# Filler matmuls on TensorE, a packed type table, and another way to the one-hot of the destination's type, in a two-layer graph network on one core

## What is computed

```
h  = relu(layernorm(x))
# layer 0: gated messages from dst to src, mean over each src, layernorm
gate = silu(edge_attr @ W1.T + b1) @ W2.T + b2
gate = gate + sum(emb[z[src]] * (emb[z[dst]] @ adaptW.T))      # z: node type, 119 kinds
msg  = gate * h[dst] * (cw(dist) * node_mult[dst])
agg  = segment_sum(msg, src) / segment_sum(node_mult[dst], src)
x    = x + layernorm(h + agg) * gamma + beta
h  = relu(layernorm(x))
# layer 1: a two-layer product for each edge, picked by the edge's type
h2   = relu(h @ weight1[rel] + bias1) @ weight2[rel]           # for h[src]
x    = x + relu(segment_sum(h2 * norm, dst) + bias2)
```

## Time and profile before

| | us |
|---|---|
| median of 3 runs | 1531.99 (1529.84 to 1539.69) |
| span of the profiled execution, first to last instruction | 1526.4 |
| stage one: first add of POOL, last add issued | 212.7, 741.6 |
| stage two: first gather, last add issued | 743.5, 1415.3 |
| last stage, loads and stores | 1418 to 1526 |
| busy over the span: PE, DVE, ACT, POOL | 1130.4, 1319.3, 668.1, 1026.1 |
| mean granted clock of PE | 0.613 of full speed |

### The profile page before, as it was taken

One profiled execution on the slowest core, in us unless ns is written; L12 is line 12 of the kernel. 1 busy time (PEld: TensorE's weight loads), 2 busy tenths in 40 slices (PEclk: granted clock), 3 DMA queues, 4 the chain that ended last, 5 costly groups with the idle time before them and its releaser, 6 DMA issues.

```text
span 1526.4 us, 20418 instructions
## 1 busy us (share of the span) xinstructions
PE 1130.4 (74%) x5198; PEld 831.4 (54%) x5198; DVE 1319.3 (86%) x3932; ACT 668.1 (44%) x1627; POOL 1026.1 (67%) x809
## 2 busy tenths in 40 slices
PE   5889899989999899881068888887878887775000
PEld 2767677777777777771035555555555555554000
DVE  6999999999989998980289999998989899888599
ACT  2444444544445444540155555555555555554000
POOL 7655667777877787566667787877777777766000
PEclk9666655655556655655575656655565556666555
DMA  7999986666666656642445666555555555554899
GB/s 225 307 324 327 328 236 157 153 146 143 142 166 149 149 139 143 155 101 11 100 120 143 166 167 156 140 138 137 136 139 127 132 131 138 138 127 81 328 400 398
DMA packets 154391, 268.73 MB, mean 176 GB/s; under 512 B 73818, under 2 KB 90411, under 8 KB 153380
## 3 DMA queue, kind: packets, MB, share of 16 engines
q1 hardware_dynamic: 78228, 223.53, 43.8%
q0 software_dynamic: 68992, 24.64, 18.5%
q10 hardware_dynamic: 7056, 19.27, 3.1%
HBM read 194.33 MB, written 112.55 MB: 201 GB/s over the span
## 4 chain that ended last, share of the span: by engine, by line
PE 34%; DVE 20%; DMA 19%; POOL 12%; issue 10%; ACT 3%; SPq 1%; POOLq 0%; DVEq 0%; ACTq 0%
PE ps_m L572 10%; POOL agg L485 8%; DMA t<-agg,src_all 6%; PE ps_m L661 6%; PE ps_qs L572 6%; DMA lows<-low 4%; PE ps_k L647 3%; DVE same L858 2%; DMA agg<-y,once 2%; DMA agg<-ysq,once 2%; DVE t L1074 2%; DVE x L1070 2%; PE ps_k L559 2%; PE ps_k L560 2%; PE ps_qs L610 1%
## 5 line engine op out<-in xcount | busy, mean ns | idle before, releaser
L521 POOL DMA_INDIRECT agg<-sums,once x196 | 312.7, 1595 | 103.5 <-issue 79.8
L443 POOL DMA_INDIRECT nodes<-in_table,dst_all x196 | 194.9, 995 | 102.2 <-issue 51.7
L512 POOL DMA_INDIRECT t<-agg,src_all x196 | 191.5, 977 | 66.1 <-issue 53.9
L572 PEld LDWEIGHTS ps_m<-msg,same 128*128 128x128 f32 x980 | 200.8, 314 | 29.0 <-issue 29.0
L572 PE MATMUL ps_m<-msg,same 128*128 128x48 f32 x980 | 208.5, 398 | 1.0 <-issue 1.0
L647 PE MATMUL ps_k<-h_t,rw_sb 56*128 56x256 f32 x588 | 122.7, 536 | 114.0 <-ACT hid L742 91.3
L572 PEld LDWEIGHTS ps_qs<-msg,same 128*128 128x128 f32 x980 | 183.6, 289 | 2.1 <-DVE msg L950 2.1
L572 PE MATMUL ps_qs<-msg,same 128*128 128x49 f32 x980 | 180.7, 363 | 2.0 <-DVE msg L950 2.0
L485 POOL DMA_INDIRECT agg<-x,once x84 | 137.4, 1635 | 43.9 <-issue 21.7
L647 PEld LDWEIGHTS ps_k<-h_t,rw_sb 56*128 56x128 f32 x588 | 62.9, 242 | 157.1 <-ACT hid L742 115.2
L559 PE MATMUL ps_k<-types_lo,low_hot 128*128 128x392 bf16 x196 | 95.7, 488 | 52.7 <-DVE low_hot L833 51.0
(11 more groups left out here) (149 smaller groups left out, 2620.2 us busy)
## 6 DMA issues: line engine op xcount, KB each, us to landing
agg<-in_both SPq DMA_DIRECT2D x14, 2758.0 KB, 15.3
t<-agg SPq DMA_DIRECT2D x49, 784.0 KB, 5.3
kept<-kept_out SPq DMA_DIRECT2D x49, 404.0 KB
kept_in<-kept SPq DMA_DIRECT2D x49, 404.0 KB, 3.5
agg<-bias_rows SPq DMA_DIRECT2D x49, 384.0 KB
out<-t ACTq DMA_DIRECT2D x49, 384.0 KB, 5.8
rows<-in_src_rows SPq DMA_DIRECT2D x49, 256.0 KB, 4.2
rows<-in_dst_rows SPq DMA_DIRECT2D x49, 256.0 KB, 3.2
```

Source lines behind the costliest of these rows:

```text
L443: pool.indirect_dma_start(nodes[s][:, t, :], None, table, bass.IndirectOffsetOnAxis(ap=dst_all[:, c:c + 1], axis=0)).then_inc(nodes_in[b % ...
L512: pool.indirect_dma_start(t2[b % T2S][:, t, :], None, wide, bass.IndirectOffsetOnAxis(ap=src_all[:, c:c + 1], axis=0)).then_inc(ends_in[b ...
L521: pool.indirect_dma_start(agg1, bass.IndirectOffsetOnAxis(ap=once1[b % LAG1][:, t:t + 1], axis=0), sums1[b % LAG1][:, t, :], None, compute ...
L572: last = mm(ps[:, t * width:(t + 1) * width], kept_same[:, at:at + P], m[:, v, :], start=(v == t), stop=(v == TILES - 1))
```

## The change

Three edits.

**The type table holds two types in a word.** Types of column n and column n + 196 are joined to one 16-bit pattern: a small multiple of 128 for the one, added to the other, with an offset that makes the bits a bf16 number. The lookup's products are 196 columns wide rather than 392, and so is `type_of`. What it accumulates is a float whose bits hold both types. DVE then shifts those bits right by 16 or 23 (`shift_all`, by whether the high part of src is at least 196), and masks 7 bits: two operations on 128x4 for each block (`zs_bits`, `zs_now`). The stored types are 8 higher than before, which `iota_type[:, ZBASE:]` takes up.

**The one-hot of z[dst] is made by PE and ACT.** DVE casts the four types of a partition to bf16 (128x4, `zd_bf`). PE multiplies each column, broadcast to 128 columns, with a bf16 identity: all rows of `ps_t` then hold the types of 128 edges. ACT squares the difference to the row's number (`apart`) and takes relu(1 - that): 1 where equal, 0 elsewhere. The 128x476 comparison of DVE (L884) and the copy of ACT (L705) are gone.

**`keep_clock`.** Products of a bf16 identity with itself, 512 columns, whose result nobody reads. In stage one there are ten for each block: three ahead of the first two lookups, one behind them, three inside `sums_within`, and one each ahead of `h1`, behind it, and behind `centred`. They write the unused bank. In stage two there are six for each round: three inside `sums_within` and three behind m1. They write `ps_k[1][:, 1]`, in which k1 has been computed; so `sums_within` now also waits for `relu1_done` of the same round.

```diff
-            types_lo = sb1("types_lo", [P, 2, NHI], BF16)
+            types_lo = sb1("types_lo", [P, 2, NPK], BF16)
...
-                pool.wait_ge(S["onehot_done"], step + 1)
+                pool.wait_ge(S["zd_done"], step + 1)
...
+            spin = ident_bf[:, :].unsqueeze(1).to_broadcast([P, TILES, P])
+
+            def keep_clock(ps, n):
+                for _ in range(n):
+                    mm(ps, ident_bf[:, :], spin, start=True, stop=True)
...
-            def sums_within(ps, width, kept_same, m):
+            def sums_within(ps, width, kept_same, m, ps_spin):
                 for t in range(TILES):
                     for v in range(t, TILES):
+                        if v == t and t > 0:
+                            keep_clock(ps_spin, 1)
...
             for b in range(NBLOCK):
+                keep_clock(ps_idle, 3)
                 if b + 1 < NBLOCK:
                     lookup(b + 1, 0)
                     lookup(b + 1, 1)
-                pe.wait_ge(S["onehot_done"], b + 1)
-                need(pe, S["onehot_t_done"], b)
+                keep_clock(ps_idle, 1)
+                pe.wait_ge(S["zd_done"], b + 1)
+                need(pe, S["apart_done"], b)
                 for t in range(TILES):
-                    last = nc.tensor.transpose(ps_t[0:NTYPE, t * P:(t + 1) * P], onehot[:, t, :], ident[:, :])
-                last.then_inc(S["turned_t_done"], 1)
+                    last = mm(ps_t[:, t * P:(t + 1) * P], zd_bf[:, t:t + 1].to_broadcast([P, P]), ident_bf[:, :], start=True, stop=True)
+                last.then_inc(S["zd_wide_done"], 1)
...
                 last.then_inc(S["gate_done"], 1)
+                keep_clock(ps_idle, 1)
                 if b + 1 < NBLOCK:
                     h1(b + 1)
+                    keep_clock(ps_idle, 1)
                     centred(b + 1)
+                    keep_clock(ps_idle, 1)
...
                     pe.wait_ge(S["m1_copied"], f + 1)
-                    sums_within(ps_sums1, H, same[f % 2], msg1).then_inc(S["sums1_done"], 1)
+                    need(pe, S["relu1_done"], min(e + 1, NBLOCK))
+                    sums_within(ps_sums1, H, same[f % 2], msg1, ps_idle1).then_inc(S["sums1_done"], 1)
...
                     last.then_inc(S["m1_done"], 1)
+                    keep_clock(ps_idle1, 3)
...
-                act.wait_ge(S["turned_t_done"], b + 1)
+                act.wait_ge(S["zd_wide_done"], b + 1)
+                A(apart[:, :], ps_t[0:NTYPE, :], ACT.Square, bias=minus_type[:, :]).then_inc(S["apart_done"], 1)
+                act.wait_ge(S["apart_done"], b + 1)
                 need(act, S["q_done"], b)
-                nc.scalar.copy(onehot_t[:, :], ps_t[0:NTYPE, :]).then_inc(S["onehot_t_done"], 1)
+                A(onehot_t[:, :], apart[:, :], ACT.Relu, scale=-1.0, bias=1.0).then_inc(S["onehot_t_done"], 1)
...
-                V.tensor_tensor(onehot[:, :, :], each(iota_type[:, :], TILES),
-                                node[:, :, H + 1:H + 2].bitcast(I32).to_broadcast([P, TILES, NTYPE]),
-                                ALU.is_equal).then_inc(S["onehot_done"], 1)
+                V.tensor_copy(zd_bf[:, :], node[:, :, H + 1:H + 2].bitcast(I32).rearrange("p t o -> p (t o)")).then_inc(S["zd_done"], 1)
...
+                dve.wait_ge(S["zsel_done"], (b + 1) * TILES)
+                V.tensor_tensor(zs_bits[:, :], zs_all[:, at:at + TILES].bitcast(I32), shift_all[:, at:at + TILES],
+                                ALU.logical_shift_right).then_inc(S["zshift_done"], 1)
...
+                V.tensor_scalar(zs_now[:, :], zs_bits[:, :], P - 1, None, ALU.bitwise_and).then_inc(S["zs_done"], 1)
```

More of the change, by code:

```diff
@@ L40 @@
 assert NHI * LO == NP
+NPK = NHI // 2
+assert NPK * 2 == NHI
+ZBASE = 8
+assert NTYPE + ZBASE <= P
 CW1 = NREL * H
@@ L207, in build @@
             hdst = sb1("hdst", [P, TILES, H])
-            onehot = sb1("onehot", [P, TILES, NTYPE])
+            zd_bf = sb1("zd_bf", [P, TILES], BF16)
+            minus_type = sb1("minus_type", [NTYPE, 1])
+            apart = sb1("apart", [NTYPE, BE])
             onehot_t = sb1("onehot_t", [NTYPE, BE])
@@ L250, in build @@
         ps_c = ps_k[0]
-        ps_l = [ps_k[1][:, a, 0:NHI] for a in range(2)]
+        ps_l = [ps_k[1][:, a, 0:NPK] for a in range(2)]
         ps_h1 = ps_m[0:H, :]
+        ps_idle = ps_k[0][:, 1, :]
+        ps_idle1 = ps_k[1][:, 1, :]
         ps_gate = ps_s[:, BE // 2:BE // 2 + TILES * H]
@@ L581, in sums0 @@
                 pe.wait_ge(S["glog_done"], b + 1)
[L582 removed]
+                sums_within(ps_s, AW, same[b % 2], msg[b % 2], ps_idle).then_inc(S["sums_done"], 1)
             h1(0)
@@ L805, in _ @@
             dve.wait_ge(S["types_in_done"], 16)
-            V.tensor_copy(types_lo[:, :, :].rearrange("p k n -> p (k n)"), types_in[:, :])
+            of_two = types_in[:, :].rearrange("p (k two n) -> p k two n", k=2, two=2)
+            V.scalar_tensor_tensor(out=types_two[:, :, :], in0=of_two[:, :, 1, :], scalar=float(P), in1=of_two[:, :, 0, :],
+                                   op0=ALU.mult, op1=ALU.add).then_inc(S["types_set"], 1)
+            dve.wait_ge(S["types_set"], 1)
+            V.tensor_scalar(types_lo[:, :, :].rearrange("p k n -> p (k n)").bitcast(U16),
+                            types_two[:, :, :].rearrange("p k n -> p (k n)"), float(ZBASE * P + ZBASE), None, ALU.add)
             dve.wait_ge(S["idx_in"], 32)
@@ L810, in _ @@
             dve.wait_ge(S["keys_set"], 2)
-            V.tensor_copy(hi_all[:, :], hi_int[:, :]).then_inc(S["keys_set"], 1)
+            V.tensor_scalar(upper[:, :], hi_int[:, :], float(NPK), None, ALU.is_ge).then_inc(S["keys_set"], 1)
+            dve.wait_ge(S["keys_set"], 3)
+            V.scalar_tensor_tensor(out=hi_all[:, :], in0=upper[:, :], scalar=-float(NPK), in1=hi_int[:, :], op0=ALU.mult,
+                                   op1=ALU.add).then_inc(S["keys_set"], 1)
+            V.tensor_scalar(shift_all[:, :], upper[:, :], 7.0, 16.0, ALU.mult, ALU.add).then_inc(S["keys_set"], 1)
             dve.wait_ge(S["pool_set"], POOL_SET)
```

37 lines of the change are left out of this document (24 added, 13 removed).

## The result

The change made the kernel slower. The changed kernel takes 1586.96 us (median of 4 runs, 1573.67 to 1592.65), the kernel before on the same chip 1530.91 us (4 runs, 1517.64 to 1539.69): a ratio of 1.0359, interval [1.0288, 1.043].

A forecast was written before the change was run, and what follows sets the result against it. POOL was taken to set stage one's end and nearly bound stage two. Gains of 3 us at the first add, 3 at stage one's end and 7 in stage two made -13: 1531.99 to 1519 us, range 1492 to 1546.

The forecast's parts named there:

- Stage one, first add: First 14 blocks, bound by DMA at share 0.98: 3 us gained, POOL's first add between 206 and 212 us.
- rival C: Fill stretch of stage one not bound by DMA, so DVE's gain arrives: -24 us, 1508 us; chance 0.12.
- End of stage one: POOL sets it; shorter blocks give some three more POOL blocks the short wait: 3 us taken, -6 with the first add.
- DVE gains 1.0 us a block: Stage one: narrower type_of and the cast replacing the comparison shorten DVE's work by 1.0 us a block, hidden behind 212 us.
- Stage two, price of the three inner fillers: Fillers between k2 and m1 add 0.7 to 1.3 us at half clock in a waiting round; 1.3 taken.
- Stage two, share of waiting rounds at full clock: Stage two: three in five waiting rounds taken to find full clock, giving -7 us over 24 pairs of rounds.
- The gain of 1.35 us a pair: Stage two: at full clock POOL takes back its wait ahead of the adds, 1.65 - 0.30 = 1.35 us.
- the hole ahead of k2: Stage two: DVE's wait for gathers leaves PE idling 3.77 us ahead of k2, which the six fillers don't fill.
- Rival D: Stage two: clock stays at half in waiting rounds, +1.3 us a pair between k2 and m1, +31 less 6, 1557 us; chance 0.14.
- a microsecond on the path costs a microsecond for each pair of rounds: Stage two: the path from gathers landed to next gathers spans two rounds, so a microsecond is half a microsecond a round.

The follow-up runs named there:

- e12_no_fillers: Changed kernel without any filler in either stage and without the wait for relu1_done: packed types and new one-hot alone; 1536.67 us, ratio 1.002 to the kernel before.
- e2_fill_two_only: Kernel before with only stage two's six fillers and the wait for relu1_done added; 1583.49 us, ratio 1.0361.
- e7_before_later: Kernel before, but SP issues the two loads of a later chunk only when the gathers in flight have landed; 1515.6 us, ratio 0.9933.
- after: The changed kernel with all three edits, against the kernel before; 1586.96 us, ratio 1.0359.
- e8_late_copy: Kernel before with one more ACT operation, a copy of 128x768 nobody reads, ahead of stage two's copy of sums; 1609.02 us, ratio 1.0547.
- e4_behind_only: Changed kernel with only the three fillers behind m1 in stage two, no inner ones and no wait for relu1_done; 1541.38 us, ratio 1.0038.
- e1_no_fill_two: Changed kernel without stage two's six fillers and the wait for relu1_done, stage one keeping all of the change; 1523.53 us, ratio 0.9972.

## Why the prediction was wrong

I predicted 1519 us in 1492 to 1546, and the median is 1586.96. By its steps:

- **Stage one, first add: inside its range, by no gain that can be told.** 211.5 us, inside 206 to 212, but the other traces on two chips have 209.9 to 213.2 with the change in stage one and 211.9 to 213.8 without; the 3 us did not come. The DMA share is still 0.98 and blocks 1 to 13 take 13.47 us against 13.55, so the gain on DVE did not arrive there, as row and bound said, and rival C is out.
- **End of stage one: the number met, by luck.** -6 us forecast, -5.7 in the one pair of traces, but no gain in the four traces with the change against the four without on the two chips above. DVE's busy time fell by 62 us where some 50 were named. But the blocks became 2.0 us shorter rather than 1.0. The last copy of sums came at 621.8 us, 70 us earlier, and POOL was 107 us late by then (its first add of the last block is at 728.78). POOL hid all of it. The step "DVE gains 1.0 us a block" priced busy time as if it were pace. Without fillers, and with PE at half clock throughout, a block gained 0.2 (`e12_no_fillers`); 1.8 came with the fillers and the clock that they brought.
- **Stage two, price of the three inner fillers: inside its bounds.** 0.7 to 1.3 us at half clock, 0.86 measured (4.50 to 5.36), 0.29 us each. The sum took 1.3, half as much again.
- **Stage two, share of waiting rounds at full clock: wrong.** "I take three in five" was 0 of 18. The gain of 1.35 us a pair that rested on it never came. The text had named the hole ahead of k2 that six fillers don't fill, and then did not let it decide. Full clock came only in rounds that don't wait (9 of 18 have fast sums), and there POOL has no use for it. The windows of the round shown above (the wait, the sums, m1; then m1 of the round before, which had no wait) have it in the column of the clock:

```profile
1250.65:1257.80 7.15, 1.08 (x4) 0.50 (x4) 3.37 (x9) 1.95 (x5) 6.24 (x4) 0.62 0.69 183
1257.80:1263.10 5.30, 5.30 (x25) 4.95 (x23) 5.26 (x20) 3.13 (x9) 4.08 (x5) 0.50 0.40 84
1263.10:1265.90 2.80, 2.80 (x13) 1.25 (x12) 2.73 (x3) 0.28 (x2) 0.16 (x1) 0.50 0.10 18
1244.80:1246.20 1.40, 1.40 (x13) 0.77 (x12) 1.36 (x8) 0.92 (x4) 1.09 (x2) 1.00 0.85 174
```

- **Stage two, what a late copy sets off: missing.** Rival D had the sign, the place and the signature (sums over 5 us, rounds over 13.3), with +31 us and 1557 us. Measured are 50.6 us. The step that failed is that a microsecond on the path costs a microsecond for each pair of rounds. A pair went from 26.48 to 28.82 us, +2.34. Of this 0.86 is the fillers and 3.82 - 2.35 = 1.47 is the landing of the gathered rows, together 2.33; that they add up so closely is partly luck, since the kernel before had 13 waiting rounds and not 18, and m1 became 0.3 us shorter. The later copy moved the last gather from 0.10 to 0.78 us behind the load's issue. The earlier trace rows showed DVE's 1.78 us of waiting, and I took it for a fixed delay of the gather. The queue of SP stood in no step of the prediction, though the loads are released by the very engine that waits.
- **That it is the loads** rests on three pairs of kernels that differ in when SP issues the two loads, and with them what stands behind them in its order, and in nothing else: 1.0359 and 1.0038 with the fillers (two chips, each beside its own kernel before; `e2_fill_two_only`, on the chip of the second, has 1.0361), 1.0547 and 1.0117 with ACT's delay, 1 and 0.9933 with neither. Landing falls from 3.82 and 4.64 us to 1.79 and 1.68.
- **Why a landing gets so long** behind 1188 KB of loads, the trace shows in good part. The gathers are on the software queue and the loads on SP's, and the rows were there 4.53 us after the wide load's issue, where the profile's page has 5.1 us as this load's own median to landing (KB, us):

```profile
t<-agg SPq DMA_DIRECT2D x49, 784.0 KB, 5.1
```

  The trace also holds every DMA record with its start, length and size. One gather is 16 records of 3136 bytes, the load of kept values 128 of 3232, the wide one 128 of 6272. Means for a block's last gather, in us from the end of its issue:

| rounds | load's first record | gather's first record | gather's last end | length of one |
|---|---|---|---|---|
| `e7_before_later`, not waiting | 2.61 | 0.71 | 1.23 | 0.25 |
| before, waiting | 1.01 | 0.70 | 2.01 | 0.56 |
| after, waiting | 0.39 | 2.06 | 3.30 | 0.17 |
| `e8_late_copy`, waiting | -0.04 | 2.63 | 4.11 | 0.14 |

  With the load a little behind, the gather starts on time and its records take twice as long. With the load ahead, the gather starts late: when its first record starts, 88 of the 128 records of kept values have started on average in `after` and 109 in `e8_late_copy`; all 128 have started in 6 and in 13 of their 18 waiting rounds. So the lateness is for the most part waiting behind the load of kept values. In one round of `after` the gather's first record came at 1.80 us though none of the load's had started, so something ahead of the transfers takes part too; what, no run shows. The Trainium skill (DMA: Bandwidth & Descriptors, section "Queues, rings and completion order") says that each DMA engine goes round the queues that have work and takes a whole packet, typically some 9 to 17 descriptors, before it changes. If a record is a descriptor and they are spread evenly, the load of kept values has 128 / 16 = 8 for each of 16 engines, so by that page the wait could be for one such packet; the trace doesn't tell which engine or packet a record belonged to, and none of the runs changed the size of the load.
- **What stays open**: why the kernel before has 13 waiting rounds, `e4_behind_only` ten and `e1_no_fill_two` none, and whether the wait for `relu1_done` adds anything alone.

## What to carry to other kernels

Before putting work on a path, look at what the end of that path releases and what other queue is released by its neighbour at about the same time: here 0.86 us on PE cost 2.3 us, as it moved the last of four small gathers behind a megabyte of loads for a later chunk. Of the 3.6% about 1% was the delay itself, which stays when the loads come later; the rest was what it set off. Fillers for the clock pay only where the clock is high in the rounds that are waited for, and where the engine behind has time to take back; read both from the trace for waiting and other rounds apart, since their mean (0.73 here) hides that the rounds that matter are at 0.5. And a load for a later block can be held back until the current block's small transfers have landed: one wait on SP gave 0.7% [0.4, 1.0] with no work removed on the kernel before, and nothing on `e1_no_fill_two`, where no round waited.

## What the runs showed of the hardware

- Four indirect gathers landed 1.5 to 1.7 us after the last one was issued with no load just ahead of them, 2.35 us when the load was issued 0.10 us ahead of the last one's end, 3.82 us at 0.78 and 4.64 us at 1.21 (means). In the last two cases the gather's first record started 2.06 and 2.63 us after the end of its issue instead of 0.7.
- Three bf16 products of 512 columns, one between each two groups of narrow fp32 products, cost 0.86 us together at half clock (0.29 each), not 0.43 each; that the rest lies beside the weight loads is not shown. At full clock throughout, the sums with their fillers take 2.84 us (9 rounds of `after`), against 4.50 us at half clock without.
- Ten such fillers in each block of stage one took the block from 13.46 us (`e12_no_fillers`, half clock throughout) to 11.66 us (`after`, clock 0.88). In stage two the clock stayed full through a wait of 2.83 us behind four fillers and fell inside the sums that followed; behind waits of 3.3 to 4.9 us the sums were at half clock from their first product in 13 of 14 rounds.
- Ahead of the first clock record of a trace the profile's clock reads 1.00: up to 39.7 us in the kernel before, whose products up to 38 us were spaced as at half clock, and through all of stage one in `e12_no_fillers`.
